# A latent-attention and expert kernel: the rows of maxima go out on ScalarE's queue as one transfer, split before their transpose, and every bulk transfer goes to SyncE's queue

## The reference

```python
xn = _layernorm(x)                       # x: 8 batches x 512 rows x 128
x = x + attn(xn) + ffn(xn)

# attn: 16 heads, each projected to a latent width L = 32
q_lat, k_lat = rope(q @ q2l_w.T + q2l_b), rope(k @ kv2l_w.T + kv2l_b)
v_lat = v @ kv2l_w.T + kv2l_b
q_for_k = q_lat @ wqk_w.T + wqk_b
att = softmax(causal(q_for_k @ k_lat.T * L ** -0.5))
y = (att @ v_lat) @ l2o_w.T + l2o_b      # then cproj_w

# ffn: a shared SwiGLU and one of 7 experts for each row (top 1 of a sigmoid router)
out = 0.5 / total_weight * shared_out + switched / total_weight
```

## Time and profile before

| | |
|---|---|
| median of 3 runs | 663.73 us (661.78 to 667.72) |
| profiled execution | 665.85 us, of which span 664.1 us |
| stages by the span | prologue to about 136 us, pipeline 136 to 564, experts 564 to 664 |
| busy share of PE, DVE, ACT, POOL | 89%, 73%, 55%, 55% |

### The profile page before, as it was taken

How to read it: one execution, slowest core, us unless ns; L and a number is a source line. 1 busy time by engine, 2 the same in 40 slices (tenths; PEclk the granted TensorE clock), 3 DMA queues, 4 the chain that set the end, 5 groups by cost and what they waited for, 6 DMA issues and landing times.

```text
span 664.1 us, 13029 instructions
## 1 busy us (share of the span) xinstructions
PE 591.9 (89%) x3642; PEld 407.4 (61%) x3642; DVE 487.2 (73%) x1707; ACT 366.8 (55%) x905; POOL 367.2 (55%) x473
## 2 busy tenths in 40 slices
PE   4679869648999799999999999989999898999993
PEld 3557657514656466666656566646656453799993
DVE  4459546337889689988999988878987568477772
ACT  5774233203767567776777766767776556322220
POOL 4000737755667557666667666657665224077775
PEclk9889979956899889999999999989999889999997
DMA  9414845474777657776877767886688962033332
GB/s 314 158 64 162 226 141 179 150 168 100 162 162 176 161 126 182 173 175 145 225 165 175 167 160 168 236 197 142 136 183 183 242 170 99 33 34 33 33 34 24
DMA packets 52692, 99.02 MB, mean 149 GB/s; under 512 B 7152, under 2 KB 28528, under 8 KB 52496
## 3 DMA queue, kind: packets, MB, share of 16 engines
q1 hardware_dynamic: 33488, 68.34, 44.2%
q10 hardware_dynamic: 11760, 22.30, 10.7%
q0 software_dynamic: 7376, 7.55, 6.5%
HBM read 27.45 MB, written 19.87 MB: 71 GB/s over the span
## 4 chain that ended last, share of the span: by engine, by line
PE 53%; DMA 9%; POOL 6%; issue 5%; DVE 2%; ACT 2%; SPq 1%; ACTq 0%; POOLq 0%; DVEq 0%
PE bank L1376 14%; PE bank L1361 13%; PE bank L1270 12%; POOL out L1110 6%; PE bank L1286 4%; PE bank L1409 4%; DMA KQ<-mxT 3%; DMA KQ<-dkq 3%; DMA out<-ye,token 2%; PE bank L1418 2%; DMA out<-xres 1%; PE bank L1393 1%; PE bank L1425 1%; ACT prob L1230 1%; DVE tk L1482 1%
## 5 line engine op out<-in xcount | busy, mean ns | idle before, releaser
L1550 DVE CUSTOM_DVE_ANT_0 scratch<-bank,late 128x512 bf16<-128x512 f32 (+3 forms) x512 | 234.4, 486 | 36.6 <-PE bank L1361 29.9
L1230 ACT ACTIVATE prob<-bank 128x512 f32<-128x512 f32 (+3 forms) x512 | 205.0, 437 | 86.2 <-PE bank L1376 84.8
L1376 PE MATMUL bank<-KQ 98*128 98x256 f32 (+2 forms) x512 | 186.6, 382 | 10.8 <-DMA KQ<-mxT 6.3
L1099 POOL TENSOR_SCALAR_AFFINE_SELECT prob<-prob 128x256 f32<-128x256 f32 x256 | 105.4, 414 | 132.4 <-ACT prob L1230 132.0
L1361 PE MATMUL bank<-KQ 96*128 96x256 f32 (+2 forms) x512 | 169.1, 380 | 2.3 <-DVE mx L1550 1.2
L1376 PEld LDWEIGHTS bank<-KQ 98*128 98x128 f32 x512 | 98.7, 195 | 77.5 <-ACT prob L1230 53.9
L1361 PEld LDWEIGHTS bank<-KQ 96*128 96x128 f32 x512 | 100.5, 199 | 58.1 <-issue 29.8
L1270 PE MATMUL bank<-prob,v_all 128*9 128x256 f32 (+3 forms) x1024 | 96.9, 454 | 0.9 <-POOL prob L1099 0.9
L1110 POOL DMA_INDIRECT out<-ye,token x38 | 59.2, 1557 | 35.2 <-DVE ye L1580 15.5
L1286 PE MATMUL bank<-stk,wl 96*128 96x512 f32 x120 | 54.1, 451 | 14.3 <-PEq L284 7.3
L351 POOL DMA_INDIRECT sorted_x<-xn,pos x32 | 31.7, 992 | 51.4 <-DVEq L805 42.7
(11 more groups left out here) (172 smaller groups left out, 953.8 us busy)
## 6 DMA issues: line engine op xcount, KB each, us to landing
KQ<-dkq SPq DMA_DIRECT2D x192, 256.0 KB, 3.9
stk<-latent ACTq DMA_DIRECT2D x42, 256.0 KB, 4.8
latent<-qkH SPq DMA_DIRECT2D x8, 512.0 KB
latent<-qkL SPq DMA_DIRECT2D x8, 512.0 KB
x<-in_x SPq DMA_DIRECT2D x12, 256.0 KB, 6.0
sorted_x<-pad_sb POOLq DMA_DIRECT2D x10, 260.0 KB, 5.2
out<-x SPq DMA_DIRECT2D x8, 256.0 KB, 2.3
KQ<-mxT SPq DMA_DIRECT2D x128, 4.0 KB
```

Source lines behind the costliest of these rows:

```text
L1099: nc.gpsimd.affine_select(out=diag, in_=diag, compare_op=ALU.is_ge, fill=0.0, base=0, pattern=[[0, 2], [1, P]], channel_multiplier=-1).the ...
L1230: nc.scalar.activation(prob[:, n % 4, cell, at:at + PW[j]], ST[i % 2][:, lo - q0:T - q0], ACT.Exp, scale=SCALE).then_inc(exp_done, 1)
L1376: nc.tensor.matmul(ST[b][:, 0:T - q0], KQ[0:SROWS, 0, n % SLOTS, T * b + P * j:T * b + P * (j + 1)], KQ[0:SROWS, 1, n % SLOTS, T * b + q0: ...
L1550: nc.vector.tensor_tensor_reduce(scratch[:, i % 2, 0:w], S[k % SBANKS][:, 0:w], mask[:, T - w:T], 1.0, MASKED, ALU.add, ALU.max, mx[:, m % ...
```

## The change

- `mx` is split on DVE, in SBUF: a rounded copy (max of the tile with itself, written as fp32r) and the difference, both 128 x 8, into `mxs` (128 x 2 x 8). TensorE transposes 128 x 16 in place of 128 x 8, after both.
- ACT copies the 16 x 128 result once, waits for its own copy, and issues one transfer into both rows of `KQ`. DVE's L1516 and SP's two transfers L1022 are gone.
- All other transfers of ACT's queue go to SP's, after the step's fills. The load of `xres` is two transfers of 256 KB, at n = 12 + 16p and 16 + 16p; the rows of n = 40 and 44 are loaded at n = 4 and 20.
- The order tables of TensorE, DVE, ACT and POOL are new. The operations in them are the same ones, except for the split.

```diff
+XRES_AT = (12, 16)
-TENSOR_ORDER = ('SSTSTTTSSTSTSTST', 'SSSTTTSTSTTSSSTT')
-MAX_T_AT, PROJECT_AT, YT_AT, LATENT_AT, SUMS_AT, OUT_AT = ((4, 3), ((6, 16), (4, 16)), (8, 14), (12, 13),
-                                                           (1, 9), (6, 5))
-VALUES_AT = {(0, 5): ((2, True, False),),
-             (0, 8): ((3, False, False),),
-             (1, 2): ((0, False, False),),
-             (1, 5): ((1, False, True),)}
-MAX_LOW_AT, OUT_ADD_AT, ROPE_AT, SUMS_USED_AT = (2, 2), (3, 3), ((5, 8), (2, 8)), 5
-MAX_HIGH_AT, Y_COPY_AT, YT_COPY_AT, HIGH_K_AT, HIGH_Q_AT = (1, 0), (1, 6), 4, ((4, 6), (3, 3)), (6, 6)
+TENSOR_ORDER = ('TSSTSTTSTSSTSSTT', 'SSTTSSTSTTSTTSST')
+MAX_T_AT, PROJECT_AT, YT_AT, LATENT_AT, SUMS_AT, OUT_AT = ((8, 3), ((3, 16), (3, 8)), (12, 13), (13, 2),
+                                                           (1, 12), (10, 6))
+VALUES_AT = {(0, 6): ((3, True, False),),
+             (1, 1): ((0, False, False),),
+             (1, 4): ((1, False, False),),
+             (1, 9): ((2, False, True),)}
+MAX_HIGH_AT, MAX_LOW_AT, OUT_ADD_AT, ROPE_AT, SUMS_USED_AT = (1, 0), (2, 0), (2, 4), ((4, 8), (2, 4)), 6
+MAX_COPY_AT, Y_COPY_AT, YT_COPY_AT, HIGH_K_AT, HIGH_Q_AT = (4, 2), (1, 7), 4, ((6, 8), (1, 4)), (6, 6)
...
         @block.sync
...
+            ROWS_AT, W2_AT = {4: 3, 20: 4, 51: 0, 53: 1, 55: 2}, 62
...
             for n in range(FIRST, LAST):
-                m = n + 1
-                if 0 <= m < STEPS:
-                    sp.wait_ge(mxT_copied, m + 1)
-                    for hl in range(2):
-                        sp.dma_start(KQ[KROWS + hl:KROWS + hl + 1, 1, m % SLOTS, :].bitcast(F32),
-                                     mxT[:, m % 2, hl, :].bitcast(F32)).then_inc(mx_in[m % 2], 16)
                 m = n + 4
...
+                if part < 3 and live(G + 1):
+                    load_latents(G + 1, part)
+                if n in ROWS_AT:
+                    load_rows(ROWS_AT[n])
+                if n in W13_AT:
+                    load_w13(slice(*W13_AT[n]))
...
+                for f in range(2):
+                    pair = (n - XRES_AT[f]) // H
+                    if (n - XRES_AT[f]) % H == 0 and 0 <= pair < PAIRS:
+                        load_residual(pair, f)
...
         @block.scalar
...
-                    if i == MAX_HIGH_AT[n % 2] and 0 <= m < STEPS:
+                    if i == MAX_COPY_AT[n % 2] and 0 <= m < STEPS:
                         act.wait_ge(mxT_ready, m + 1)
                         if m >= 2:
-                            act.wait_ge(mx_in[m % 2], 32 * (m // 2))
-                        nc.scalar.copy(mxT[:, m % 2, 0, :], MXT).then_inc(mxT_high, 1)
+                            act.wait_ge(mx_in[m % 2], 16 * (m // 2))
+                        nc.scalar.copy(mxT[:, m % 2, :], MXT).then_inc(mxT_copied, 1)
+                        act.wait_ge(mxT_copied, m + 1)
+                        act.dma_start(KQ[KROWS:SROWS, 1, m % SLOTS, :].bitcast(F32).rearrange("h (s c) -> h s c", c=P),
+                                      mxT[:, m % 2, :].bitcast(F32)).then_inc(mx_in[m % 2], 16)
...
         @block.tensor
...
                     if at == MAX_T_AT[n % 2] and 0 <= m < STEPS:
-                        pe.wait_ge(s_max, 8 * m + 8)
+                        pe.wait_ge(mx_split, m + 1)
                         m_free()
-                        nc.tensor.transpose(MXT, mx[:, m % 2, :], ident).then_inc(mxT_ready, 1)
+                        nc.tensor.transpose(MXT, mxs[:, m % 2, :, :].rearrange("p h k -> p (h k)").bitcast(F32), ident
+                                            ).then_inc(mxT_ready, 1)
...
         @block.vector
...
-                    if i == MAX_LOW_AT[n % 2] and 0 <= m < STEPS:
-                        dve.wait_ge(mxT_high, m + 1)
-                        nc.vector.tensor_tensor(mxT[:, m % 2, 1, :], MXT, mxT[:, m % 2, 0, :].bitcast(F32),
-                                                ALU.subtract).then_inc(mxT_copied, 1)
+                    if i == MAX_HIGH_AT[n % 2] and 0 <= m < STEPS:
+                        dve.wait_ge(s_max, 8 * m + 8)
...
+                        nc.vector.tensor_tensor(mxs[:, m % 2, 0, :], mx[:, m % 2, :], mx[:, m % 2, :], ALU.max
+                                                ).then_inc(mx_high, 1)
...
+                    if i == MAX_LOW_AT[n % 2] and 0 <= m < STEPS:
+                        dve.wait_ge(mx_high, m + 1)
+                        nc.vector.tensor_tensor(mxs[:, m % 2, 1, :], mx[:, m % 2, :], mxs[:, m % 2, 0, :].bitcast(F32),
+                                                ALU.subtract).then_inc(mx_split, 1)
```

More of the change, by code:

```diff
@@ L926, in attention @@
     mx = sb("mx", [P, 2, 2 * QT], F32)
-    mxT = sb("mxT", [2 * QT, 2, 2, P], F32R)
+    mxs = sb("mxs", [P, 2, 2, 2 * QT], F32R)
+    mxT = sb("mxT", [4 * QT, 2, P], F32R)
     rz = sb("rz", [P, 2 * QT, 2], F32)
@@ L1016, in _, with load_latents, load_residual, load_rows @@
         def _(sp):
-            for n in range(FIRST, LAST):
-                m = n + 1
-                if 0 <= m < STEPS:
-                    sp.wait_ge(mxT_copied, m + 1)
-                    for hl in range(2):
-                        sp.dma_start(KQ[KROWS + hl:KROWS + hl + 1, 1, m % SLOTS, :].bitcast(F32),
-                                     mxT[:, m % 2, hl, :].bitcast(F32)).then_inc(mx_in[m % 2], 16)
+            def load_latents(G, r):
+                pair, g = G // G_PER_PAIR, G % G_PER_PAIR
+                if G >= 3 and r == 0:
+                    sp.wait_ge(pa_ready, 8 * (G - 2))
+                sp.dma_start(stk[L * r:L * (r + 1), G % 2, :, :].bitcast(F32),
+                             latent[(0, 0, 1)[r], :, L * g:L * (g + 1), PT * pair:PT * (pair + 1)
+                                    ].rearrange("k i n -> i k n")).then_inc(stk_in[G % 2], 16)
+            def load_residual(pair, f):
+                if pair:
+                    sp.wait_ge(mixed_out, 16 * pair)
+                rows = slice(PT * pair + T * f, PT * pair + T * (f + 1))
+                sp.dma_start(xres[:, QT * f:QT * (f + 1), :], out[rows, :].rearrange("(p t) c -> p t c", t=QT)
+                              ).then_inc(xres_in, 16)
+            def load_rows(i):
+                if i == 0:
+                    sp.wait_ge(pv_done, H // 2 * (PAIRS - 1))
+                sp.dma_start((xs_early[:, XW * i:XW * (i + 1)] if i < XV else
+                               xs_late[:, XW * (i - XV):XW * (i + 1 - XV)]), xs_rows[:, XW * i:XW * (i + 1), :]
+                              ).then_inc(xs_in[i], 16)
+            def load_w13(es):
+                if es.start == 0:
+                    sp.wait_ge(pa_ready, 8 * GROUPS - 8)
+                    sp.wait_ge(kl_ready, 2 * GROUPS - 2)
+                    sp.wait_ge(wq_ready, 2 * GROUPS - 2)
+                    sp.wait_ge(ql_ready, 2 * GROUPS - 2)
+                sp.dma_start(w13[:, es, :], d["w13"][:, es, :]).then_inc(w13_in[W13_PART[es.start]], 16)
+            ROWS_AT, W2_AT = {4: 3, 20: 4, 51: 0, 53: 1, 55: 2}, 62
+            for n in range(FIRST, LAST):
                 m = n + 4
@@ L1036, in _ @@
                                      dkq[rows, parts, g % 2, :].bitcast(F32)).then_inc(filled[slot], 16)
+                G, part = chunk(n)
+                if part < 3 and live(G + 1):
[4 more added lines that the diff above has]
+                    load_w13(slice(*W13_AT[n]))
+                if n == W2_AT:
+                    sp.dma_start(w2[:], d["w2"]).then_inc(w2_in, 16)
+                if n % H == 8 and 0 <= n - H < STEPS:
+                    pair = n // H - 1
+                    sp.wait_ge(o_added, 2 * pair + 2)
+                    sp.dma_start(out[PT * pair:PT * (pair + 1), :].rearrange("(f p t) c -> p f (t c)", f=2, t=QT),
+                                 xres[:].rearrange("p (f t) c -> p f (t c)", f=2)).then_inc(mixed_out, 16)
+                for f in range(2):
+                    pair = (n - XRES_AT[f]) // H
+                    if (n - XRES_AT[f]) % H == 0 and 0 <= pair < PAIRS:
+                        load_residual(pair, f)
             for half in range(2):
@@ L1124, in high_k @@
                 nc.scalar.copy(dkq[:, KH, G % 2, half], tk1[:, half]).then_inc(kh_ready, 1)
[L1126 to L1133, removed]
             def copy_xT(t):
@@ L1520, in _ @@
                         dve.wait_ge(out_ready, 2 * pair + f + 1)
-                        dve.wait_ge(xres_in, 16 * (pair + 1))
+                        dve.wait_ge(xres_in, 16 * (2 * pair + 2))
                         rows = xres[:, QT * f:QT * (f + 1), :].rearrange("p t c -> p (t c)")
```

54 lines of the change are left out of this document (12 added, 42 removed).

## The result

The kernel before takes 665.62 us (661.78 to 667.72), the changed one **691.06 us** (688.93 to 695.05). The ratio is 1.040, with an interval of 1.032 to 1.047: slower by 4%. The forecast was 652 us. The profiled execution of the changed kernel took 688.93 us, of which the span is 687.2 (before: 664.1).

A forecast was written before the change was run, and what follows sets the result against it. TensorE was taken as the bound, with no idle time in undisturbed two-step windows (11.65 us a pair). Transfer terms -6 - 3 - 1 - 2 = -12, 0 for the rest, gave 663.7 - 12 = 652 us; range 638 to 678.

The forecast's parts named there:

- the long windows: Six two-step windows, 16.5 us in all above the steady pace of 11.65; the changed transfers were to win 12.
- The split on DVE: DVE busy 3.7 us more in 64 steps, its waiting falling by more; PE feels neither: 0, between -2 and +3.
- Is the row in time?: Transpose to next step's first T: odd to even stays 4.8 us; even to odd 4.0, 2.4 left for landing, just in time.
- That rival: Row of maxima lands late in every even step, behind fills and latents: 667 to 703 us, middle 680; chance 0.15.
- ACT's issue: ACT issues the row's transfer, 0.65 us each, 1.3 a pair: taken as 0, bad end 0.6 us a pair (18 us).
- Bulk on SP and halves: ACT's other transfers moved to SP, residual in halves: -6 - 3 - 1 - 2 = -12 us over the long windows.
- the first pair of long windows: Windows where the 512 KB residual load was in flight, 7.5 us, should go for the most part: -6.
- the one with the late fill: Window where a fill cost 3.9 us; with bulk on SP the fill is on time: -3 (0 to -3.9).
- the one at 413.50: The long window at 413.50 was to give -1 us.
- the last two: Last two long windows, 3.9 us, with expert weights still in flight, so half: -2.
- ScalarE's wait for fills: ACT's wait for fills, counted with the latents' issue as 9.7 us in all, 11 times, was to be lost.
- Bulk on SP costs issue time: SP loses 1.43 us of issue a step and gains some 0.44 for latents.

The follow-up runs named there:

- experiment 7: experiment 3 with two of GpSimd's additions one place later in its order: 646.5 us, ratio 0.985 to the kernel before.
- experiment 3: The changed kernel with the row of maxima issued by SP ahead of its fills, in one transfer, ACT only copying: 666.9 us, ratio 1.016 to the kernel before.
- experiment 12: The kernel before with only the residual loaded in two halves, at n = 12 and 16, still on ACT's queue: 653.3 us, ratio 0.985.
- experiment 1: The changed kernel with SP waiting for the copy of the row of maxima before it issues the step's fills: 678.2 us, ratio 1.031 to the kernel before.
- experiment 8: The changed kernel, ACT issuing the row, with only GpSimd's two additions one place later: 675.2 us, ratio 1.025 to the kernel before.
- experiment 9: The changed kernel, ACT issuing the row, with GpSimd's two additions one place later and the fills held back: 661.5 us, ratio 1.011 to the kernel before.
- experiment 11: The kernel before with all bulk on SP behind the fills, residual in halves, row loads at 4 and 20: 657.8 us, ratio 0.987.
- experiment 2: The changed kernel with ACT issuing the row's high and low half as two transfers of 8 x 128: 718.1 us, ratio 1.090 to the kernel before.
- experiment 6: experiment 3 with the transpose of odd steps' maxima one place later (place 4 instead of 3): 675.9 us, ratio 1.018 to the kernel before.

## Why the prediction was wrong

Three terms make up the result, and the runs price each against the form of experiment 7, 0.985. The split in GpSimd's way: 1.016 - 0.985 = 3.1%, 20 us. The row on ACT's queue behind fills and other bulk instead of on SP's ahead of them: 1.025 - 0.985 = 4.0%, 26 us. Both together, the changed kernel, 1.040: 5.5%, 36 us, less than the sum of 46. They overlap: in the changed kernel the split's first operation is busy for 23.6 us, against 37.2 in experiment 3, so it stands behind GpSimd for less. I had forecast -12 us for the long windows and 0 for all else; 1.5% or 10 us is what experiment 7 and experiment 12 keep.

- **The split on DVE, costed at 0: the step that failed first.** The sum of durations was right for a free engine (0.16 us measured, 0.167 taken from the earlier trace rows). But the row I took was of a single instruction in the prologue, beside which GpSimd did nothing. In the loop GpSimd is busy for 7 to 9.5 us of a pair, and the split stood still while one of its additions ran. DVE loses up to 1.02 us in each pair, of which it had 0.9 free. I had also looked at the odd steps, where the split was on time; the transpose that waited was that in even steps. My range for this term, -2 to +3 us, was wrong by 17.
- **Is the row in time? The step that failed second.** I left 2.4 us for landing in the even-to-odd passage and took the other one for safe, with 4.8 us. Measured is the reverse: rows of even steps, whose passage I had taken for safe, were late 16 times of 19, those of odd steps 6 times. From an odd step's transpose the copy waits in ACT's order, and it is 1.18 + 0.62 us to the end of the issue; 3.0 us are left and the row needs 3.70. From an even step's it is 0.62 + 0.62, leaving 3.2, and it needs 3.07. I took the landing from rows that were posted ahead of the fills, 2.47 us at most, though the change posts them behind fills and other bulk. The rows said what a row takes among other transfers, 2.9 to 4.1 us behind its issue, and that range holds both medians. I used them for a rival with 0.15 when they were the nearest rows for the new order. And bulk on SP, which I counted as won, puts the latents between the fills and the row. By the rows compared in experiment 1 this is the larger part of its lateness, though no run shows it by itself.
- **That rival** (row late in every even step, 667 to 703, middle 680) gave the time and half of the mechanism: the row was late, but mostly in the other passage. The late row alone, experiment 8 at 1.025, would be 682 us here; the rest up to 691 is the split, which this rival did not have. Its rate, 3 us for each 0.1 us, was right in kind: 0.7 us too long a landing would give 21 us by it, and the row costs 26.
- **ACT's issue, costed at 0 with 0.6 us a pair as the bad end: right at 0.** It took 0.62 us, and in experiment 9 the steady pair is at the old pace with it.
- **Bulk on SP and halves, -12 in all: right in size.** From the kernel before to experiment 7 the first pair of long windows gives 7.3 us (I had 6), the one with the late fill 3.7 (3), the one at 413.50 0.9 (1), the last two 1.7 (2). Six windows with the attention output take 3.4 us back, so 10 are left. That most of it lay in the halves and not in the queue, I had not separated: with the halves alone, of these windows only that of the late fill stays long, 13.8 us.
- **ScalarE's wait for fills** (9.7 us, 11 times) is gone in the changed kernel, as I had said. In experiment 11, with the old tables, it is 11.3 us, 12 times.
- **Bulk on SP costs issue time.** The latents' issue took 0.31 us on ACT and takes 1.27 us on SP behind the fills, which is 0.95 a step (three steps of four) and not the 0.44 I had added. SP had room for it.
- **The start of the loop, not costed at all.** The first four steps lost 5.3 us, and that is the row: their two pairs take 30.1 us in the changed kernel and 29.9 in experiment 8, which has the late row alone, against 25.4 in experiment 3, 24.7 in experiment 7 and 24.8 before. The granted clock there is 0.72 and 0.79, as it falls to its lower level once more behind the idle time of the first pair. Of the 3.0 us ahead of the first T, 2.0 are there when the first transpose begins (161.5 against 159.5 us), ahead of any row; their cause stays open.

The Trainium skill's rule that I had weighed against the sum ("DMA: Bandwidth & Descriptors", "Issuing engines are not separate DMA queues") held: queues of two issuing engines share the DMA engines. A queue of its own gave the row no shelter here: by the medians it landed in 1.28 to 2.20 us when SP posted it ahead of the fills (experiments 3 and 7), and in 2.67 to 3.70 on ACT's queue beside or behind them (experiments 2, 8, 9 and the changed kernel).

The rule that I missed stands there too. The Trainium skill ("SBUF — State Buffer", "SBUF: two separate sides") says that VectorE and GpSimd share a pair of SBUF ports under an exclusive lock, and that a VectorE operation with both inputs in SBUF takes it against a GpSimd operation that reads SBUF, one of them then standing still for the whole instruction of the other. The trace agrees: 1.18 us instead of 0.16, ending within 0.03 us of GpSimd's end. The subtraction of before had its first input in PSUM and took 271 to 280 ns in all 64 cases, though 37 of them ran wholly within a tensor_tensor of GpSimd; the new one has both inputs in SBUF.

## What to carry to other kernels

A duration taken from a quiet stretch is the price of an operation alone. Where an operation changes the memories that it reads, look at which engine shares its way there and lay its place in the order beside that engine's, not only beside its own. A small transfer's landing is to be read from rows that stand in the same order to the bulk as it will: 8 KB posted just behind fills and latents, and no longer ahead of them, cost 26 us, and ACT's issue of them nothing that shows in the steady pairs. And try the smallest part of a change alone: here the two halves of one transfer hold all the gain, and all else had to be mended with two entries of GpSimd's table only to be as fast.

## What the runs showed of the hardware

- DVE's tensor_tensor of 128 x 8 with two SBUF inputs: 0.16 us free, up to 1.25 us beside a GpSimd tensor_tensor of 128 x 512 (1.28 us; experiments 3 and 6), up to 0.41 us beside an affine_select (0.41 us). GpSimd's own addition took 1.27 us (median) in experiment 3 and 1.28 in 7. Reading one input from PSUM it showed no such wait: 271 to 280 ns, 64 times, 37 of them wholly within a GpSimd tensor_tensor.
- The same 8 KB within SBUF, issued once: landed in 1.3 to 2.2 us (medians) ahead of 768 KB of fills, 2.7 to 2.9 us when both were posted at the same time from two engines, 1.3 to 2.4 us behind the fills alone (six rows), and 3.6 us (median of 51 rows) behind fills and the 256 KB or more that the same engine posted next.
- An issue's own time depends on what its engine has just posted: 256 KB of latents took SP's sequencer 0.32 us in the two cases in which it stood behind nothing, and 1.27 us (median of 38) just behind three fills; on ACT, behind nothing, 0.31 us.
